# Hybrid attention, scan and expert kernel: q and k of all heads turned once in the mixture and laid out through DRAM, values weighed head by head

## The reference, cut to what matters

```python
q, k, v = to_heads(split(x @ qkv_w + qkv_b))          # 16 heads, 8 channels
q = apply_rotary(q); k = apply_rotary(k)
weights = softmax(einsum('bhqd,bhkd->bhqk', q, k) * SCALE)
attn = einsum('bhqk,bhkd->bhqd', weights, v)          # then @ out_w + out_b
```

## Time and profile before

| | us |
|---|---|
| median of 3 runs | 10301.96 (10301.13 to 10309.9) |
| the profiled execution, its own time | 10288.07 |
| its span in the profile | 10285.8 |
| busy: PE, DVE, ACT, POOL | 9253.0, 8862.1, 7235.6, 6118.4 |

### The profile page before, as it was taken

How to read it: one execution, slowest core, us unless ns; L and a number is a source line. 1 busy time by engine, 2 the same in 40 slices (tenths; PEclk the granted TensorE clock), 3 DMA queues, 4 the chain that set the end, 5 groups by cost and what they waited for, 6 DMA issues and landing times.

```text
span 10285.8 us, 259086 instructions
## 1 busy us (share of the span) xinstructions
PE 9253.0 (90%) x88474; PEld 6391.3 (62%) x88474; DVE 8862.1 (86%) x16781; ACT 7235.6 (70%) x15052; POOL 6118.4 (59%) x4900
## 2 busy tenths in 40 slices
PE   7989899898998989989899899999989999899988
PEld 4656656566565665656656566565665656656566
DVE  6988979789797897978979799797997979879798
ACT  5867768677686776857768576685866858668586
POOL 1936829377293772927729277392763928639286
PEclk9999999999999999999999999999999999999999
DMA  0000000000000000000000000000000000000000
GB/s 22 0 3 1 2 3 0 3 1 2 3 0 3 1 2 3 0 3 1 2 3 0 3 1 2 3 0 3 1 2 3 0 3 1 2 3 0 3 1 3
DMA packets 648478, 23.66 MB, mean 2 GB/s; under 512 B 629185, under 2 KB 647250, under 8 KB 647506
## 3 DMA queue, kind: packets, MB, share of 16 engines
q1 hardware_dynamic: 647890, 16.11, 3.7%
HBM read 9.40 MB, written 4.19 MB: 1 GB/s over the span
## 4 chain that ended last, share of the span: by engine, by line
DVE 28%; PE 23%; issue 18%; POOL 17%; ACT 11%; DVEq 1%; POOLq 1%; DMA 0%; SPq 0%; ACTq 0%
POOL work L1714 16%; DVE work L1605 11%; DVE work L1595 6%; PE ps L605 4%; ACT scan_in L1099 4%; PE ps L595 4%; PE ps L590 3%; PE ps L534 3%; PE ps L522 2%; DVE stats L1225 1%; ACT da L985 1%; ACT yscT L1132 1%; DVE scan_in L1509 1%; POOL skip_u L1687 1%; PE ps L802 1%
## 5 line engine op out<-in xcount | busy, mean ns | idle before, releaser
L1714 POOL TENSOR_TENSOR work<-work,crep 128x512 f32<-128x512 f32 x4608 | 5765.1, 1277 | 4093.7 <-DVE work L1544 3590.7
L1099 ACT ACTIVATE scan_in<-du,bcn 128x256 f32<-128x256 f32 x8832 | 3690.6, 497 | 69.6 <-PE ps L812 36.9
L1605 DVE TENSOR_TENSOR_SCAN work<-da,hend,ps 128x256 f32<-128x256 f32 x4608 | 3028.0, 725 | 57.8 <-PE ps L812 48.7
L812 PE MATMUL ps<-w_ident,scan_in 128*128 128x128 f32 x18432 | 2455.3, 278 | 275.6 <-ACT scan_in L1099 147.0
L812 PEld LDWEIGHTS ps<-w_ident,scan_in 128*128 128x128 f32 x18432 | 2018.9, 142 | 873.6 <-DVE work L1605 324.6
L1595 DVE TENSOR_TENSOR_SCAN work<-da,ps 128x512 f32<-128x512 f32 x2048 | 2353.4, 1201 | 38.8
L802 PE MATMUL ps<-work,w_sel 128*32 128x256 f32 x17792 | 1408.7, 390 | 276.5 <-POOL work L1714 275.5
L1020 ACT ACTIVATE work<-ps,w_gate_b 128x512 f32<-128x512 f32 x512 | 349.6, 686 | 824.7 <-PE ps L590 684.4
L802 PEld LDWEIGHTS ps<-work,w_sel 128*32 128x32 f32 x17792 | 375.3, 108 | 756.7 <-POOL work L1714 541.3
L1336 DVE TENSOR_REDUCE smax<-ps 128x1 f32<-128x512 f32 x1024 | 656.9, 685 | 162.0 <-PE ps L499 158.0
L985 ACT ACTIVATE da<-ps 128x512 f32<-128x512 f32 x1024 | 555.3, 606 | 147.3 <-PE ps L522 140.4
(11 more groups left out here) (205 smaller groups left out, 12083.1 us busy)
## 6 DMA issues: line engine op xcount, KB each, us to landing
hend<-work SPq DMA_DIRECT2D x2304, 1.0 KB, 1.8
x_in<-in_x SPq DMA_DIRECT2D x17, 256.0 KB, 2.8
out<-work SPq DMA_DIRECT2D x16, 256.0 KB
gate_w<-in_gate_w SPq DMA_DIRECT2D x1, 1024.0 KB, 5.0
up_w<-in_up_w SPq DMA_DIRECT2D x1, 1024.0 KB, 7.1
down_w<-in_down_w SPq DMA_DIRECT2D x1, 1024.0 KB, 9.1
w_w_zy<-in_w_zy SPq DMA_DIRECT2D x1, 256.0 KB
work<-in_w_mix SPq DMA_DIRECT2D x1, 256.0 KB
```

The lines of the kernel that those rows point to most:

```text
L812: mm = eng.transpose(ps[:, bank, c:c + P], scan_in[:, m, tb, 2 * j + s].rearrange("p k c -> p (k c)"), ident[:])
L1099: ins = eng.activation(scan_in[:, m, tb, :, k, :], du[:, hf, tb, :].rearrange("p (e c) -> p e c", c=GC), ACT.Copy, scale=bcn[:, hf, tb, 0, ...
L1605: ins = eng.tensor_tensor_scan(hst[:, p % NHID, half], da[:, 1, 2 * p + s, :], ps[:, RING[p % 4], half], hend[:, 2 * p + s:2 * p + s + 1], ...
L1714: eng.tensor_tensor(prod[:, to, :].rearrange("p (s t) -> p s t", s=2), hst[:, p % NHID, :].rearrange("p (s t) -> p s t", s=2), crep[:, hf, ...
```

## The change

Steps of the preparation are moved and rewritten. PE makes q, k, v at the beginning of the second mixture, in place of 20 of the 24 dummies; DVE takes them between norm and router, and rotates behind the hides 1 and 3. The rotated q and k now lie by channel and head, so behind expert 0 eight f32 transposes turn all heads at once into two PSUM banks; the three parts are made in that layout by ACT (steps 2, 3 behind half experts 5 and 7) and DVE (7 and 8 behind experts 1 and 2). The values' clearing and x with bias go behind expert 3. SP stores the parts to DRAM (5 stores of 256 KB, two parts twice) and loads them as score rows of 24 partitions, 8 heads wide: 12 loads of 192 KB, and 4 loads of constant rows that replace the clearing. Both halves of the heads have a semaphore. All 16 heads lie in SBUF; the turning and copying of each head are gone. `weigh` is done for each head, its four key blocks side by side and three heads in one bank, and `turn_out` sums the key blocks by a product with `sel`, into bank 6; so there are 6 outputs in place of 4, and 2 banks for rescores in place of 3. All maxima are copied by ACT. Removed lines of long blocks, and changes of counts and declarations, are left out here:

```diff
-HG = 4
+HG = 3
+HR = 4
+OUTS = -(-NH // HG)
+HC = HD + 1
...
-K_SLOTS = ((5, 7), (1, 8), (2, 4))
-QUAD = 4
+HALVES = 2
+HH = NH // HALVES
...
-RESCORE = (3, 4, 6)
+RESCORE = (3, 4)
+QKV_BANK = (6, 2)
 MAX_AT = 3
-PE_START, ACT_START = (1, 2), (11, 13, 15)
-DVE_START = ((0, 2), (3,), (4, 5), (6,), (7,), (8,), (), (9,))
+PE_ROT = 0
+ACT_START = (5, 7)
+DVE_START = ((), (7,), (8,), (0, 2), (), (), (), (9,))
+WEIGH_AT = 3
+STORES = (0, 1, 2, 0, 1)
...
+parts_d = nc.dram_tensor("parts_d", (len(STORES), 2, P, T), BF16, kind="Internal").ap()
+pad_d = nc.dram_tensor("pad_d", (2, BIAS + 2 - QR, T), BF16, kind="Internal").ap()
...
+heads_flat = piece(NH * 2 * T // 2)
+heads = heads_flat.bitcast(BF16).rearrange("p (k h t) -> p k h t", h=NH, k=2)
+probsT = piece(HR * TB * T).rearrange("p (j k t) -> p j k t", j=HR, k=TB)
...
+parts = third[:, 6144:7680].bitcast(BF16).rearrange("p (n s t) -> p n s t", n=PARTS, s=2)
+xnT_next = third[:, 7680:8192]
+left = scr[:, 2560:3584].rearrange("p (s t) -> p s t", s=2)
...
+rot_t = ps[:, 4:6, :]
...
+    def load_heads(at, step=0):
+        eng.wait_ge(qkv_taken.sem, qkv_taken.count(at, 1))
+        for g in range(HALVES):
+            for k, rows in enumerate((BIAS - QR, BIAS + 2 - QR)):
+                eng.dma_start(
+                    heads[QR:QR + rows, k, g * HH:(g + 1) * HH, :],
+                    pad_d[k, 0:rows].rearrange("r (o t) -> r o t", o=1).broadcast_to([rows, HH, T])
+                    ).then_inc(heads_in[g].sem, heads_in[g].up(at))
+        for n, part in ((0, 0), (3, 0), (1, 1), (4, 1), (2, 2)):
+            if part < PARTS - 1:
+                eng.wait_ge(part_a.sem, part_a.count(at, part + 1))
+            else:
+                eng.wait_ge(part_v.sem, part_v.count(at, 1))
+            eng.dma_start(parts_d[n].rearrange("s p t -> p s t"), parts[:, part]
+                          ).then_inc(parts_kept.sem, parts_kept.up(at))
+        eng.wait_ge(parts_kept.sem, parts_kept.last(at))
+        by_kind = parts_d.rearrange("n s (c k h) t -> k (n s c) h t", k=2, h=NH)
+        for g in range(HALVES):
+            for k in range(2):
+                for r in range(PARTS):
+                    first = HD * r if k else 0
+                    eng.dma_start(
+                        heads[HD * PARTS * r:HD * PARTS * (r + 1), k, g * HH:(g + 1) * HH, :],
+                        by_kind[k, first:first + HD * PARTS, g * HH:(g + 1) * HH, :]
+                        ).then_inc(heads_in[g].sem, heads_in[g].up(at))
...
     with eng.Fori(0, B - 1) as b:
         loop_ends(b)
         eng.wait_ge(x_free.sem, b + 1)
         eng.dma_start(x_in[:], x_t[b + 1]).then_inc(x_loaded.sem, 16)
+        load_heads(Place(b + 1, 0))
...
+            first = QKV_BANK[step - 1]
             if step == 1:
                 eng.wait_ge(n_att.xnT.sem, n_att.xnT.count(at, 1))
...
             for k in range(2):
                 tb = 2 * (step - 1) + k
-                mm = eng.matmul(ps[:, 4 + k, 0:3 * DM], xnT_next[:, tb * P:(tb + 1) * P],
+                mm = eng.matmul(ps[:, first + k, 0:3 * DM], xnT_next[:, tb * P:(tb + 1) * P],
                                 w["qkv_w"][:], start=True, stop=True)
             mm.then_inc(qkv_done.sem, qkv_done.up(at))
+        if step == 3:
+            eng.wait_ge(rot_done.sem, rot_done.count(at, 1))
+            for part in range(2):
+                for tb in range(TB):
+                    mm = eng.transpose(rot_t[:, part, tb * P:(tb + 1) * P],
+                                       rot[:, tb, part * P:(part + 1) * P], ident[:])
+            mm.then_inc(rot_turned.sem, rot_turned.up(at))
...
         def score(h, qb):
             u = TB * h + qb
...
+            if qb == 0 and h % HH == 0:
+                eng.wait_ge(heads_in[h // HH].sem, heads_in[h // HH].count(at, 2 * PARTS + 2))
             if u >= 3:
                 eng.wait_ge(maxed.sem, maxed.count(at, u - 2))
-            q, k = heads[0:BIAS, h % QUAD, 0], heads[0:BIAS, h % QUAD, 1]
+            q, k = heads[0:BIAS, 0, h], heads[0:BIAS, 1, h]
...
+            if u >= 2:
+                eng.wait_ge(exped.sem, exped.count(at, u - 1))
+            q, k = heads[0:BIAS + 2, 0, h], heads[0:BIAS + 2, 1, h]
+            mm = eng.matmul(bank(RESCORE[u % 2]), k[:, kb * P:(kb + 1) * P], q,
                             start=True, stop=True)
             mm.then_inc(rescored.sem, rescored.up(at))
...
+        def weigh(h):
+            eng.wait_ge(exped.sem, exped.count(at, TB * (h + 1)))
+            if h == 0:
                 eng.wait_ge(v_ready.sem, v_ready.count(at, 1))
...
+            if h > 0 and h % HG == 0:
+                eng.wait_ge(o_copied.sem, o_copied.count(at, h // HG))
+            for kb in range(TB):
+                mm = eng.matmul(ps[32 * kb:32 * kb + 32, 7, :],
+                                vaug[:, kb, h, :], probsT[:, h % HR, kb, :],
+                                start=(h % HG == 0), stop=(h % HG == HG - 1 or h == NH - 1))
             mm.then_inc(weighed.sem, weighed.up(at))
         def turn_out(c):
             eng.wait_ge(o_copied.sem, o_copied.count(at, c + 1))
+            if c > 0:
+                eng.wait_ge(o_normed.sem, o_normed.count(at, c))
             for tb in range(TB):
-                mm = eng.transpose(blocks(7)[:, tb, :], oT[:, tb * P:(tb + 1) * P], ident[:])
+                mm = eng.matmul(ps[:, 6, tb * GC:(tb + 1) * GC], oT[:, tb * P:(tb + 1) * P],
+                                w["sel"][:], start=(tb == 0), stop=(tb == TB - 1))
             mm.then_inc(o_turned.sem, o_turned.up(at))
-        keep_busy(1, 0)
-        turn_head(0)
-        keep_busy(8, 0)
-        turn_head(1)
-        for h in range(NH + AHEAD + 2):
+        for h in range(NH + AHEAD):
             behind = h - AHEAD
             for b in range(TB):
                 if h < NH:
                     score(h, b)
                 if b == MAX_AT - 1 and 1 <= h <= NH:
                     turn_max(h - 1)
...
                 if 0 <= behind < NH:
                     rescore(behind, b)
...
+                if b == WEIGH_AT and behind >= 1:
+                    weigh(behind - 1)
+            if behind >= HG + 1 and behind % HG == 1:
                 turn_out(behind // HG - 1)
-        eng.wait_ge(o_normed.sem, o_normed.count(at, NH // HG))
+        weigh(NH - 1)
...
     def mixture(at, coming=None):
-        keep_busy(24, 1)
+        if coming is None:
+            keep_busy(24, 1)
+        else:
+            start(coming, 1)
+            eng.wait_ge(x3_ready.sem, x3_ready.count(at, 1))
+            start(coming, 2)
+            keep_busy(4, 1)
...
+        if coming is not None:
+            eng.wait_ge(qkv_taken.sem, qkv_taken.count(coming, 2))
...
-            if coming is not None and e in PE_START:
+            if coming is not None and e == PE_ROT:
                 eng.wait_ge(summed.sem, summed.count(at, 1))
-                start(coming, 1 + PE_START.index(e))
+                start(coming, 3)
...
+        if step == 2:
+            eng.wait_ge(rot_turned.sem, rot_turned.count(at, 1))
+            eng.activation(parts[:, 0], rot_t, ACT.Copy).then_inc(part_a.sem, part_a.up(at))
+        if step == 3:
+            eng.wait_ge(left_done.sem, left_done.count(at, 1))
+            eng.activation(parts[:, 1], left, ACT.Copy).then_inc(part_a.sem, part_a.up(at))
...
         def exp(h, kb):
             eng.wait_ge(rescored.sem, rescored.count(at, TB * h + kb + 1))
...
+            if h >= HR and kb == 0:
+                eng.wait_ge(weighed.sem, weighed.count(at, h - HR + 1))
+            eng.activation(probsT[:, h % HR, kb, :], bank(RESCORE[(TB * h + kb) % 2]), ACT.Exp,
                            scale=SCALE).then_inc(exped.sem, exped.up(at))
         def copy_out(c):
-            eng.wait_ge(weighed.sem, weighed.count(at, TB * (c + 1)))
+            eng.wait_ge(weighed.sem, weighed.count(at, min(HG * (c + 1), NH)))
+            if c > 0:
+                eng.wait_ge(o_turned.sem, o_turned.count(at, c))
             eng.activation(oT, bank(7), ACT.Copy).then_inc(o_copied.sem, o_copied.up(at))
         eng.activation(exp_one[:], one[:], ACT.Exp)
...
+        for h in range(NH + AHEAD):
             behind = h - AHEAD
             for b in range(TB):
-                if b == MAX_AT and 1 <= h <= NH and h % 2 == 0:
+                if b == MAX_AT and 1 <= h <= NH:
                     copy_max(h - 1)
                 if 0 <= behind < NH:
                     exp(behind, b)
             if behind >= HG and behind % HG == 0:
                 copy_out(behind // HG - 1)
...
+        copy_out(OUTS - 1)
...
-        if step == 5:
+        if step in (5, 6):
+            half = step - 5
...
-            r = rot.rearrange("p b (h two j) -> p two b h j", two=2, j=4)
+            r = rot.rearrange("p b (two j h) -> p two b h j", two=2, j=4)
...
+            first, second, op = ((even, odd, ALU.subtract), (odd, even, ALU.add))[half]
+            if half == 1:
```

(40 more changed lines are left out.)

154 lines of the change are left out of this document (32 added, 122 removed).

## The result

The changed kernel takes 10245.85 us (median of 5 runs, 10244.34 to 10248.81); the kernel before took 10301.96 (10289.36 to 10309.9 over 5 runs beside it). The ratio is 0.9948, 95% interval 0.9934 to 0.9961: half a per cent faster, where 1.3% was forecast. The profiled execution took 10245.85 us with a span of 10243.8, so 42.0 us of span were gained against the profiled 10285.8, not 133.

A forecast was written before the change was run, and what follows sets the result against it. Attention heads were taken as paced by DVE three times in four, else PE; the mixture by PE. Per sequence 2.7 + 6.2 - 1.0 = 7.9, times 16 is 126, plus 12, minus 5: 133 us off, giving 10168 us, range 10085 to 10220.

The forecast's parts named there:

- the clock: First heads of the attention: too little PE work lowers the clock, costing 1.0 us a sequence, bounds 0 and 3.
- The scans: Scan turns, some 450 us of a sequence's 640: taken as untouched by the change.
- The second mixture: Mixture preparing the next q and k: 3.6 us removed, 0.9 added, gain 2.7 us a sequence, bounds 1.3 and 3.2.
- the eight transposes: f32 transposes of turned q and k in the second mixture: 0.9 us added, bounds half and double.
- The start of the attention: From PE's last expert product to the first row maximum: gain 0.8 us, 15 times, bounds 0 and 2.7.
- The loop: Attention's loop over heads: PE sets the pace at 3.3 us a head; attention 67.6 against 73.8, gain 6.2 us.
- an output turning: Attention output turned by a product instead of a transpose: 0.88 us each, lower bound 0.44.
- Sequence 1: First sequence: nothing hides its chain of parts and loads, a loss of 5 us (0 to 12).
- (a): Rival, attention loop: tighter coupling with two rescore banks, PE waits 0.3 us a head; 10251 us, chance 0.17.
- The heads from DRAM: Loads of heads ahead of the attention: cost 0, landed at 671 to 673, some 10 us of room.
- (b): Rival, first score: 24-row loads need 4 us each, heads land at 694, PE waits 12 us; 10348 us, chance 0.07.
- (c): Rival, inside the attention loop: small PE idles drop the clock, loop grows 11 us; 10344 us, chance 0.08.

The follow-up runs named there:

- e5: Changed kernel plus f32 fillers: 4 ahead of the first score, 2, 2 and 1 behind each score of heads 0 to 2, 17 in the tail; 10168.31 us.
- e10: Changed kernel plus 3, 6 and 10 f32 fillers ahead of the last three sums of the last scan unit; 10216.23 us.
- e12: Kernel before plus f32 fillers: 8 and 4 in the attention's tail, 3, 6 and 10 in the last scan unit; 10270.19 us.
- e6: Changed kernel plus two more bf16 score products behind each score of heads 0 to 2; 10239.38 us.
- e7: Changed kernel plus eight bf16 products of the identity behind each score of heads 0 to 2; 10226.1 us.
- e1: Changed kernel plus 3, 3 and 2 f32 fillers behind the scores of heads 0, 1 and 2; 10217.4 us.
- e2: Changed kernel with the loads of heads 8 to 15 issued behind the store of the output; 10259.92 us.
- e3: Kernel before without its nine f32 fillers at the attention's start; 10295.32 us, ratio 0.9997.

## Why the prediction was wrong

The direction was right, the gain 2.4 times too large (133 us against 56 in medians, 42 in spans).

**The step that failed is the clock.** It took 1.0 us a sequence, with 3 as the upper bound, "because scores at 1.2 GHz still keep up with DVE and only head 2 or 3 pays". Scores alone keep up. But from head 2 on PE also rescores, and eight products 0.42 us apart and a turning need 4 us where DVE needs 2.8; the stretch went on to the first weighing, in the turn of head 3 (702.38). Start of head 14's rescores: 58.1 us behind the first row maximum (747.89), not 54.5, so 3.6 us; e5, warm, gives 3.1 of these back by the last head's row maximum (50.7 for 53.8). Another 0.9 us lie in the projection. That is about 4.5 us instead of 1.0, 56 us in all. The same comes out from the other side: where the clock holds, e5's attention takes 67.68 us, 4.6 less than the 72.29 of the change, and the forecast was 67.6.

The step also asked only what the clock costs inside the changed code. The scans, "untouched", became 1.8 us a sequence longer, 29 us. The cold time from the last scan unit on rose from 2.6 to 5.8 us a sequence in the profiled executions, and with the same fillers there the two kernels are level (e10 505.54, e12 505.65). That this is a matter of where the falls happen to lie shows in e6 and e7, whose edits in the attention alone brought the stretch back to 506.3 us. 56 and 29 are 85 of the 91 us missing in the spans.

**The rest of the sum held.** The second mixture gained 3.04 us (forecast 2.7), with the eight transposes at 0.88 us, the value of their nearest row. The start of the attention gained 0.41, not 0.8: PE's idle time doubled, and DVE's own turn round the loop is some 2.5 us (e1's first row maximum waits for "issue" while the scores lie ready). The loop is 3.27 us a head for 3.3, an output turning 0.91 for 0.88, and PE never waits within the warm heads. Sequence 1 lost 6.6 us for 5. The recorded text names two spans, its own range of 10085 to 10220 and ends of 10090 and 10260 that take in (a); the 10246 lie outside the first.

**The heads from DRAM** cost nothing, as said, with about the room that was said, but later and slower. The last store landed at 670.6, not 666, and SP issued the loads right behind it:

```profile
670.62 4.80 SPq L454 DMA_DIRECT2D da<-parts_d  x12
```

The 12 loads then move 2.36 MB from 671.6 to 685.8, 166 GB/s, DMA share 0.75 (window above), where 280 GB/s were taken. The six for heads 0 to 7, for which alone the first score waits, had landed at 679.7, not 671 to 673, but 8.8 us ahead of the score at 688.50; those for heads 8 to 15 landed at 686.6, and head 8 is half an attention away. The Trainium skill's rule ("DMA: Bandwidth & Descriptors", on why a DMA increments its semaphore by 16), by which 24 rows use 12 of 16 engines, agrees with the share of 0.75; the estimate worked out from it, 5.6 us for six loads, is a fifth short of the 7.1 that half of the stretch makes. What was not on the list at all is what the traffic does to "issue".

**Rivals.** (a) gave 10251, near the result, by a mechanism that isn't there: two banks cost PE nothing in 43.00 busy of 43.00 us. (b) didn't occur, six loads taking 7 us and not 24; its sum is off besides, since six loads of 4 us from 666 end at 690, not 694. (c) placed the clock inside the loop, by small idles: it was at the head, from too little work, and a third of the size. The Trainium skill's rule of the cycling banks ("TensorE: Matmul & The Clock Gate", A second HAM failure mode: psum-queue depth-cycling) doesn't show here either: two banks cycle at granted 1.00.

Open: that "issue" is instruction fetch behind the loads' traffic fits e2, in which the stall moved with the traffic, but no row names a fetch. Why the cold stretch lasts 3 us in one sequence and 7 in the next of the same kernel isn't settled either.

## What to carry to other kernels

When a change removes work from PE, price the clock for every product that then runs cold, through to the place where PE is filled again, and look at it in all stages, the untouched ones too; dummy products in the waits of the first iterations and of the tail (here 4 ahead of the first score, 8, 8 and 4 in the first three heads, 17 in the tail) gave back 78 us, 67 of them in the attention. Don't put a gain down to the stage that was edited before the other stages have been measured: e6 and e7 gained only elsewhere. Compare with the old kernel given the same fillers, before you credit the change. And a transfer that is hidden from the data's side may still hold up the engines' issue at a loop's end: read the rows that begin with "issue" around it.

## What was not expected of the hardware

A window of the changed kernel in the cold stretch of sequence 2, before the first weighing:

```profile
695.00:702.00 7.00, 6.98 (x23) 1.90 (x20) 5.31 (x12) 4.54 (x8) 0.00 (x0) 0.50 0.00 0
```

- Seven microseconds of nearly gapless bf16 products in the changed kernel did not raise the granted clock from 0.50 (PE busy 6.98 of 7.00 us), while the kernel before without fillers was back at 1.00 by 1.7 to 4.9 us behind the first row maximum with light, mixed work (e3), and two more products per score did it by 4.7 to 10.8 us (e6).
- With the loads under way ACT's idle time "issue" at the loop's end is 5.6 us a turn (84.7 over 15), 1.9 with half of them elsewhere (29.0, e2), and 1.2 in the kernel before, which has no such loads (17.5).
- Removing all of the start's fillers from the kernel before cost nothing measurable (0.9997), though cold time rose from 3.8 to 9.2 us per attention.
- Work in the first three heads of the attention also changed the stage behind it: mixture 1 and scans took 508.03 us in the changed kernel and 506.26 and 506.33 in e6 and e7, with the same code there.
